# Another order in the main attention: value products two score tiles apart, prepared blocks behind a unit's first tile

## The reference, cut to what matters

```python
qf = jnp.concatenate([q_nope, q_pe], -1)
kf = jnp.concatenate([k_nope, k_pe], -1)
scores = jnp.einsum('bhqd,bhkd->bhqk', qf, kf) * scale
probs = jax.nn.softmax(scores.astype(jnp.float32), axis=-1).astype(dt)
ctx = jnp.einsum('bhqk,bhkd->bhqd', probs, v)
main_out = ctx.transpose(0, 2, 1, 3).reshape(b, s, H * D_V) @ o_w.T
...
return gates[..., 0:1] * main_out + gates[..., 1:2] * pattern_out
```

## Time and profile before

| | before |
|---|---|
| median of the runs | 1260.73 us |
| the profiled execution, its own time | 1260.88 us |
| its span, first to last instruction | 1259.0 us |
| TensorE products busy | 1177.3 us (94%) |
| VectorE busy | 890.4 us (71%) |
| ScalarE busy | 654.0 us (52%) |
| GpSimd busy | 532.2 us (42%) |
| mean granted TensorE clock | 0.979 |

### The profile page before, as it was taken

How to read it: one execution, slowest core, us unless ns; L and a number is a source line. 1 busy time by engine, 2 the same in 40 slices (tenths; PEclk the granted TensorE clock), 3 DMA queues, 4 the chain that set the end, 5 groups by cost and what they waited for, 6 DMA issues and landing times.

```text
span 1259.0 us, 34623 instructions
## 1 busy us (share of the span) xinstructions
PE 1177.3 (94%) x14433; PEld 825.6 (66%) x14436; DVE 890.4 (71%) x1354; ACT 654.0 (52%) x1242; POOL 532.2 (42%) x531
## 2 busy tenths in 40 slices
PE   8999999999899999999998789999998998989997
PEld 5643434467677777777776577888653444778997
DVE  4689988448688887887788947456777753766555
ACT  3579988854344444444444334332455775345553
POOL 4256265325958777696764034452100000412221
PEclk8999999999899999999999889999999998899999
DMA  7870000011111111111111040110335100101111
GB/s 282 217 171 15 2 18 16 13 34 43 30 41 38 32 34 42 39 32 32 41 32 62 11 147 1 51 52 12 88 89 124 45 9 1 34 18 42 48 38 34
DMA packets 41699, 66.25 MB, mean 53 GB/s; under 512 B 8476, under 2 KB 27676, under 8 KB 40604
## 3 DMA queue, kind: packets, MB, share of 16 engines
q1 hardware_dynamic: 41544, 64.04, 18.8%
HBM read 45.60 MB, written 8.45 MB: 43 GB/s over the span
## 4 chain that ended last, share of the span: by engine, by line
PE 72%; DVE 14%; issue 4%; ACT 4%; POOL 3%; DMA 1%; SPq 1%; DVEq 0%; ACTq 0%; POOLq 0%
PE bank L1478 8%; PE bank L1938 7%; PE bank L2148 6%; PE bank L2149 6%; PE bank L2150 6%; PE bank L1569 5%; PE bank L1435 4%; PE bank L1834 4%; PE bank L1836 3%; PE bank L1835 3%; PE bank L1972 3%; PE bank L1298 3%; PE bank L1415 2%; DVE mpc L1377 2%; DVE nmq L1843 2%
## 5 line engine op out<-in xcount | busy, mean ns | idle before, releaser
L1456 ACT ACTIVATE Pb<-bank 128x512 f32<-128x512 f32 (+3 forms) x355 | 180.6, 574 | 29.7 <-PE bank L1435 8.9
L1843 DVE TENSOR_REDUCE nmq<-bank 128x1 f32<-128x1024 f32 x128 | 154.7, 1209 | 53.8 <-PE bank L1836 53.2
L1858 ACT ACTIVATE P<-bank,nmq 128x1024 f32<-128x1024 f32 x128 | 142.7, 1115 | 93.6 <-DVE nmq L1843 92.8
L1306 DVE TENSOR_REDUCE mp<-bank 128x2 f32<-128x1024 f32 x128 | 153.5, 1222 | 27.3 <-PE bank L1298 26.6
L1871 DVE STREAM_TRANSPOSE PT<-P 128x1024 f32<-128x1024 f32 x124 | 151.7, 1224 | 0.0
L1938 PE MATMUL bank<-PT,kv 32*64 32x128 f32 x7936 | 137.2, 276 | 11.7 <-issue 11.0
L1938 PEld LDWEIGHTS bank<-PT,kv 32*64 32x64 f32 x7936 | 118.7, 131 | 37.9 <-issue 37.8
L1377 DVE TENSOR_REDUCE mpc<-bank 128x2 f32<-128x1024 f32 (+2 forms) x96 | 88.3, 953 | 44.7 <-PE bank L1365 22.1
L1834 PE MATMUL bank<-qk1h,qk0h 128*128 128x512 f32 x256 | 111.5, 436 | 8.6 <-POOL qk0l L1676 4.0
L1478 PE MATMUL bank<-Pb,vx 128*17 128x256 f32 (+3 forms) x1222 | 107.2, 410 | 0.6 <-ACT OTa L1492 0.5
L1836 PE MATMUL bank<-qk1h,qk0l 128*128 128x512 f32 x256 | 101.9, 398 | 0.1
(11 more groups left out here) (354 smaller groups left out, 2881.2 us busy)
## 6 DMA issues: line engine op xcount, KB each, us to landing
t<-t SPq DMA_DIRECT2D x128, 64.0 KB, 2.4
wr<-wf SPq DMA_DIRECT2D x25, 256.0 KB, 2.7
wraw<-wf SPq DMA_DIRECT2D x8, 768.0 KB, 4.5
scratch<-stgr SPq DMA_DIRECT2D x4, 1024.0 KB, 4.0
Rs<-shares SPq DMA_DIRECT2D x64, 64.0 KB, 2.8
scratch<-stg SPq DMA_DIRECT2D x8, 384.0 KB, 2.6
qst<-scratch SPq DMA_DIRECT2D x9, 256.0 KB, 8.3
owT<-owT SPq DMA_DIRECT2D x1, 2048.0 KB, 11.6
```

The lines of the kernel that those rows point to most:

```text
L1306: e.tensor_reduce(mp[:, w % 3, :, j, kh], wide[slot][:], AX, ALU.max).then_inc(ring_ok, 1)
L1456: e.activation(PBR[l][i % len(PBR[l])][:, 0:c], bank[b][:, 0:c], ACT.Exp, scale=0.25).then_inc(exp_ok[0], 1)
L1843: e.tensor_reduce(nmq[:, n % 8:n % 8 + 1], scores(u, i), AX, ALU.max, negate=True).then_inc(mp_ok, 1)
L1858: e.activation(probabilities(u, i)[:], scores(u, i), ACT.Exp, bias=nmq[:, n % 8:n % 8 + 1], accum_out=sums[:, u % 2, i:i + 1]).then_inc(ex ...
```

## The change

It rewrites `PREP_AT` to count in units and puts all of a unit's blocks behind its tile 0: each block's product behind the projection, each copy behind exp 0. The spread moves behind the copies (and so, on SyncE, behind their swaps). The first value piece moves from behind score 2 to behind score 1. Exp 3 moves ahead of lift on ScalarE. VectorE's own order stays as it was. Of pair 1, the second block moves from unit 2 to unit 1, else each block stays in its unit.

```diff
--- before.py
+++ after.py
@@ -72,7 +72,7 @@
     (31, 1): [("normed", 0)],
 }
 
-PREP_AT = ((5, 8, 9, 12, 13, 16),) + ((1, 5, 9, 12, 13, 16),) * 6
+PREP_AT = ((1, 1, 2, 3, 3, 4),) + ((0, 1, 2, 3, 3, 4),) * 6
 
 
 def main_order():
@@ -80,11 +80,13 @@
     order = [("expo", 0, 1), ("score", 0, 2), ("ctx", 0), ("ctx", 1), ("vturn", 0, 0), ("expo", 0, 2), ("score", 0, 3),
              ("cadd", 0), ("ctx", 2), ("vturn", 0, 1), ("cadd", 1), ("expo", 0, 3), ("ctx", 3), ("cadd", 2), ("vturn", 0, 2),
              ("cadd", 3)]
-    preps = {16 * (p - 1) + at: (p, i) for p in range(1, 8) for i, at in enumerate(PREP_AT[p - 1])}
-
-    def prep(n, kind):
-        if n in preps:
-            order.append((kind, *preps[n]))
+    preps = {}
+    for p in range(1, 8):
+        for i, at in enumerate(PREP_AT[p - 1]):
+            preps.setdefault(4 * (p - 1) + at, []).append((p, i))
+
+    def prep(u, kind):
+        order.extend((kind, *block) for block in preps.get(u, ()))
 
     def output(u):
         if u >= 0:
@@ -93,17 +95,15 @@
     for u in range(1, 32):
         order.append(("score", u, 0))
         output(u - 2)
-        prep(4 * u, "prep")
-        order.extend([("rec", u - 1), ("spread", u - 1), ("vturn", u - 1, 3), ("expo", u, 0)])
-        prep(4 * u, "pcopy")
+        prep(u, "prep")
+        order.extend([("rec", u - 1), ("vturn", u - 1, 3), ("expo", u, 0)])
+        prep(u, "pcopy")
+        order.append(("spread", u - 1))
         order.extend(BESIDE_LAST.get((u, 0), ()))
-        order.append(("score", u, 1))
-        prep(4 * u + 1, "prep")
-        prep(4 * u + 1, "pcopy")
-        order.extend([("vturn", u, 0), ("expo", u, 1)])
+        order.extend([("score", u, 1), ("pv", u - 1, 0), ("vturn", u, 0), ("expo", u, 1)])
         order.extend(BESIDE_LAST.get((u, 1), ()))
-        order.extend([("score", u, 2), ("pv", u - 1, 0), ("vturn", u, 1), ("expo", u, 2)])
-        order.extend([("score", u, 3), ("pv", u - 1, 1), ("lift", u - 1), ("vturn", u, 2), ("ot", u - 1), ("expo", u, 3)])
+        order.extend([("score", u, 2), ("vturn", u, 1), ("expo", u, 2)])
+        order.extend([("score", u, 3), ("pv", u - 1, 1), ("expo", u, 3), ("lift", u - 1), ("vturn", u, 2), ("ot", u - 1)])
     output(30)
     order.extend([("rec", 31), ("spread", 31), ("vturn", 31, 3), ("turn", 0), ("pv", 31, 0), ("pv", 31, 1), ("hT", 0),
                   ("wup", 1), ("wdown", 1), ("lift", 31), ("ot", 31), ("project", 31), ("logits", 0), ("add", 31)])
```

## The result

The changed kernel takes 1296.14 us (median; 1295.28 to 1299.45) against 1260.82 us beside it: 1.0292 times as long (95% interval 1.0271 to 1.0312), 35 us slower. The forecast was 1294 us in a range of 1277 to 1311, slower with a chance of 0.91.

The account below looks back on a forecast made before the run. TensorE leads, VectorE close behind, and the loop closes through the projection. Thirty units at +1.3 us plus 2.4 and 2.8 give 44.2; less 11.1 in credits, +33.1 on 1260.9 makes 1294 us, range 1277 to 1311.

Parts of the forecast that it names:

- a): Loop from score 2 through maximum 3, exp 3 and lift to the projection: 8.22 us, adding 1.3 us a unit.
- E: The moment on TensorE when value piece 0 ends and score 2 can start; later steps are timed from it.
- b): Value piece 0 waits for VectorE's turn 3: +2.8 us over 14 units with one block, +2.4 in unit 30.
- c): Blocks behind tile 0, swaps ahead of spread: GpSimd stop goes, -4.0 us, its clock fall -1.6; late spread costs nothing.
- d): Instruction holes in second value pieces on TensorE: 5.5 us absorbed by the time to spare before lift.
- The clock rival: TensorE's regular waits of 1.7 us lower its clock in 15 units: 1317 us, chance 0.10.
- The spread rival: On SyncE the spread lands late, so OTm waits for it instead of lift: 1314 us, chance 0.05.
- The fast rival: On ScalarE exp 3 doesn't hold lift, the loop stays bound by TensorE: 1239 to 1250, say 1247 us; chance 0.06.

Follow-up runs that it names:

- X: Only exp 3 moved ahead of lift on ScalarE, against the kernel before: 1270.9 us, ratio 1.0107.
- B: Only the blocks moved behind tile 0 and the spread behind the copies, against the kernel before: 1256.6 us, ratio 0.9996.
- V: Only value piece 0 moved behind score 1, against the kernel before: 1284.9 us, ratio 1.0204.
- the faster versions: Kernel before with blocks and spread moved, exp 3 ahead of lift, projection behind score 1: 1267.5 us; also add ahead of maximum 1: 1249.7 us.

## Why the prediction was right, step by step

**a) The loop through score 2: right, term by term.** 8.22 us were worked out from E to the projection, 8.28 were found. Units with two blocks grew by the forecast 1.3 us (the shortest with ten products for its blocks, from 13.76 to 15.04). That this loop is the cause is shown by three runs that each shorten one link: maximum 3 without the transpose ahead of it (-22 us, 18 to 27 expected), lift ahead of exp 3 (1269.9, 1269 expected), piece 0 behind score 2 (1263.3, 1267 expected). The two parts strengthen each other: X costs 14 us alone (1256.7 to 1270.9) and 24 with B and V in place (1269.9 to 1294.0; 28 by the ratios, since the two were measured at different times), because exp 3 delays lift only as far as maximum 3 is late itself. A unit shows it too: X adds 0.4 us alone (13.76 to 14.15) and 1.1 with B and V (13.92 to 15.04).

**b) Turn 3 before piece 0: right and small.** TensorE's products waited four times for a turned tile, 3.8 us in all; 2.8 for the units with one block and 1.1 for unit 30 were reckoned. The units with one block grew by 1.6 us (12.81 to 14.4) where those with two grew by 1.3, so the term was nearer 0.3 us a unit than 0.2.

**c) Blocks and spread: the stop of 4.0 us at GpSimd went as forecast, and the spread cost next to nothing at these units (0.4 us).** What I didn't see is what the moved blocks are for. I costed the two moves each against the kernel before and found B nearly free. That is true, but without B, value piece 0 would have stood right behind a block's product and waited 0.9 us for its copy. The forecast holds since both moves were made together.

**d) Holes: wrong, and the slow stretch was priced too low.** Of the holes, 5.5 us were to be absorbed. TensorE's products waited 11.6 us inside value pieces with no semaphore named, in 7 places; over the same view the kernel before has 12.3 in 12, and the changed kernel measured once more has 9.3 in 7. The holes went from pairs to single long ones, and six of the seven stand in piece 0, which is in the loop, where nothing absorbs them. Only the seventh, 1.7 us in piece 1, was absorbed in part: TensorE's next wait for OTm was 0.7 us instead of 2.0. Here is the hole that cost most, and the clock behind it:

```profile
558.97 0.98 PE L1938 MATMUL bank<-PT,kv 32*64 32x128 f32 x26 [1.91 <-issue]
...
560.00:565.00 5.00, 5.00 (x73) 3.88 (x78) 2.18 (x2) 0.92 (x1) 4.27 (x6) 0.74 0.12 30
```

That unit, with two blocks, took 18.9 us from projection to projection (550.52 to 569.39) where others of its kind take 15.1: the hole is 1.9 us, and the lower clock (0.92 and 0.74 in the two stretches of 5 us) comes to 1.7. It is no new cost: the kernel before has such a stretch behind its hole at 583 us, 0.83 over 580 to 590, also 1.7 us. The credited stretch is another one, behind the stop at GpSimd, and it did go. I had priced it by the one at 585 us, at 1.6 us; its own row says more:

```profile
320.00:330.00 10.00, 6.93 (x19) 5.53 (x20) 4.30 (x8) 2.96 (x5) 9.27 (x11) 0.66 0.00 0
```

0.34 of 10 us are 3.4 us. The two units that held the stop and this stretch took 19.2 and 15.7 us in the kernel before, where others of their kinds take 13.8 and 14.0: 7.1 us in all, where the forecast has 5.6.

**The sum again, from projection to projection.** The growth of the units comes to about 45.3 us (37.5 in 26 units, 4.9 in the last three, 3.0 ahead of them), where a) and b) have 44.2. The stop takes off 7.1 instead of 5.6. Holes and the other slow stretches take off about 2.2, which I get as the remainder, instead of 5.5. That is the 36.0 us by which the stretch from the score tile behind the pattern attention (265.68 us before, 264.38 after) to the last projection (730.62 and 765.35) grew in the two profiled executions. Their spans differ by 35.9. So 1294 came this close because a) was right and the other errors partly offset each other: 3.3 us of holes missing and 1.1 us more growth stand against 1.5 us more for the stop.

**The rivals.** The clock rival did not come as told: TensorE's weight loads idle 2.0 us ahead of 30 projections, its products 1.6, and the mean clock is 0.981 against 0.979. But it came once, behind the first of these waits:

```profile
292.20 1.36 PE L1972 MATMUL bank<-mo,OTm 128*128 128x256 f32 x4 [1.96 <-DVE OTm L1963]
...
292.00:297.00 5.00, 4.80 (x14) 3.87 (x15) 3.61 (x7) 1.80 (x3) 4.69 (x4) 0.66 0.01 2
```

A grant of 0.66 over 5 us is 1.7 us; the repeat of the changed kernel has the same fall (0.83 over 290 to 300), the kernel before has none there. The other waits did no harm: from 300 to 750 us, seen in steps of 10 us, the granted clock is below 1.00 only in the two steps from 550 to 570 (0.96, 0.87), behind the 1.9 us hole. The spread rival is refuted for the changed kernel by the run with the spread ahead (1295.4), but was real in the faster versions. The fast rival fails on the row of maximum 3, E+4.00.

## What to carry to other kernels

When a step moves ahead in one engine's order, write down what now stands behind it on that engine and follow those to the end of the loop: value piece 0 was 2 us early, and score 2, which everything else hung on, 2 us late. Two moves must be priced together, since one may be the repair of the other (B measured 0 us alone and 17 with V and X). And an engine that stops at the same step each time is best helped by giving it what is ready first, with whatever gates the next step (here the add on VectorE) moved along: without that second half the same idea lost 11 us, with it, it won 6.

## What was not expected of the hardware

Holes in which TensorE waits within a run of small products, with no semaphore named, come in all of these orders, mostly 40 to 60 us apart with a few longer gaps, single ones up to 2.2 us long. They do not go away when TensorE has 1.6 us of idle time in each unit: 12.3 us in the kernel before, 11.6 in the changed one, 11.4 in the run with maximum 3 ahead. Their sum varies (9.3 in the repeat of the changed kernel, 7.9 with B alone, 8.1 with B and X, 6.6 with V and X), so a few us of difference say little. Their places do not vary: the changed kernel, its repeat and the runs with lift back, with the spread ahead and with maximum 3 ahead have one order on TensorE, and in all five the long holes stand 26, 18, 11, 26, 14 and 6 products before the end of a value piece 0, in that sequence, though their times differ by up to 24 us. So a hole's place goes with TensorE's instructions and not with the time. That would fit a supply of instructions in large portions; no run here varied the number of instructions, so that stays an inference.
